# Five 64-row second parts and the skip term on the full height of the array, in a fused ConvNeXt and selective-scan kernel

## The reference, cut to what matters

```
xz = ln(silu(norm(x))) @ in_proj_w;  xc, z = split(xz)      # 192 channels each (DN)
xc = silu(conv3x3(xc) + conv_b)
xs = four orders of xc's 64 pixels (K = 4)
x_dbl = einsum('bkdl,kcd->bkcl', xs, x_proj_w)              # sum over the 192 channels
delta = softplus(dts @ dt_w + dt_b);  A = -exp(A_logs)
h = h * exp(delta * A) + (delta * u) * B;  y = sum_n h * C  # 16 states per channel
y = y + D * xs;  y = y0 + y1 + y2 + y3                      # D * xs is the skip term
y = ln(y) * silu(z);  out = y @ out_proj_w                  # mean, variance and product over 192 channels
```

## Time and profile before

| | |
|---|---|
| time, median of 3 runs | 31036.96 us (31032.65 to 31046.93) |
| span of the profiled execution | 31035.4 us |
| what lies around the span, by the median | 1.6 us |
| TensorE matmuls busy | 28615.5 us, 92% |
| VectorE busy | 27602.9 us, 89% |
| ScalarE busy | 24152.4 us, 78% |
| GpSimd busy | 25853.7 us, 83% |
| mean granted TensorE clock | 0.991 |

### The profile page before, as it was taken

One profiled execution on the slowest core, in us unless ns is written; L12 is line 12 of the kernel. 1 busy time (PEld: TensorE's weight loads), 2 busy tenths in 40 slices (PEclk: granted clock), 3 DMA queues, 4 the chain that ended last, 5 costly groups with the idle time before them and its releaser, 6 DMA issues.

```text
span 31035.4 us, 986155 instructions
## 1 busy us (share of the span) xinstructions
PE 28615.5 (92%) x399070; PEld 10807.2 (35%) x399070; DVE 27602.9 (89%) x18447; ACT 24152.4 (78%) x37826; POOL 25853.7 (83%) x13288
## 2 busy tenths in 40 slices
PE   8999799999999999999999999999999999999998
PEld 2333233333333333333333333333333333333333
DVE  7888799999999999999999999999999999999998
ACT  4555688888888888888888888888888888888887
POOL 0000599999999999999999999999999999999999
PEclk9999999999999999999999999999999999999999
DMA  3333344444444444444444444444444444444444
GB/s 82 88 84 82 79 103 99 102 98 102 99 101 100 100 100 100 101 100 102 99 102 100 101 99 101 99 103 98 103 98 102 100 102 99 102 98 102 98 102 90
DMA packets 3821867, 3043.32 MB, mean 98 GB/s; under 512 B 2184848, under 2 KB 2987792, under 8 KB 3796944
## 3 DMA queue, kind: packets, MB, share of 16 engines
q1 hardware_dynamic: 3809888, 2910.77, 44.4%
q0 software_dynamic: 8560, 77.41, 0.7%
HBM read 2325.71 MB, written 449.58 MB: 89 GB/s over the span
## 4 chain that ended last, share of the span: by engine, by line
PE 28%; POOL 20%; issue 18%; ACT 13%; DVE 8%; DMA 1%; POOLq 0%; SPq 0%; ACTq 0%; DVEq 0%
POOL state L942 17%; PE dbu L1032 9%; PE pp L1126 7%; DVE state L1477 5%; ACT state L1256 5%; PE yb L1051 4%; DVE dg L1467 2%; PE pp L1100 2%; POOL dd L949 2%; PE pp L1089 1%; PE pp L1120 1%; ACT sp_w L1333 1%; POOL dd L962 1%; ACT sp_v L1334 1%; PE b_t L1068 1%
## 5 line engine op out<-in xcount | busy, mean ns | idle before, releaser
L942 POOL TENSOR_TENSOR state<-state,cc 128x1024 f32<-128x1024 f32 x9408 | 22044.2, 2375 | 1411.5 <-DVE state L1477 1381.9
L1477 DVE TENSOR_TENSOR_SCAN state<-state,dbu 128x1024 f32<-128x1024 f32 x9408 | 21000.9, 2269 | 2295.8 <-PE dbu L1032 2292.6
L1256 ACT ACTIVATE state<-dl,a_neg 128x512 f32<-128x512 f32 x18816 | 12250.6, 711 | 21.2 <-DMA dl<-dlx 1.4
L1032 PE MATMUL dbu<-dg,du_t 64*32 64x256 f32 x301056 | 10198.2, 383 | 968.5 <-DVE state L1477 895.6
L1032 PEld LDWEIGHTS dbu<-dg,du_t 64*32 64x32 f32 x301056 | 5100.0, 106 | 7276.9 <-issue 6198.1
L1051 PE MATMUL yb<-state,mask 128*32 128x512 f32 x37632 | 5078.5, 612 | 2.2 <-POOL state L942 2.2
L1467 DVE TENSOR_TENSOR dg<-b_t,mask_q 128x1024 f32<-128x1024 f32 x3136 | 3757.7, 1198 | 41.4 <-PE b_t L1068 41.4
L229 POOL DMA_DIRECT2D act_d<-acted x32 | 16.3, 509 | 3218.2 <-DVE mixed L489 2909.2
L1126 PE MATMUL pp<-sp_a,minus 128*128 128x512 f32 x2352 | 1321.4, 644 | 587.4 <-ACT ye L1284 252.1
L1339 ACT ACTIVATE sp_y<-pp 128x512 f32<-128x512 f32 x1176 | 704.2, 599 | 1440.4 <-PE pp L1126 1417.1
L437 DVE SCALAR_TENSOR_TENSOR acc<-image,cw_v,acc 96x432 f32<-96x432 f32 (+2 forms) x2912 | 1687.6, 647 | 0.0
(11 more groups left out here) (174 smaller groups left out, 26584.2 us busy)
## 6 DMA issues: line engine op xcount, KB each, us to landing
dl<-dlx SPq DMA_DIRECT2D x4704, 256.0 KB, 4.7
cc<-cd SPq DMA_DIRECT2D x3136, 256.0 KB, 6.2
dlx<-dd SPq DMA_DIRECT2D x1176, 256.0 KB, 2.0
shifted<-in_x SPq DMA_DIRECT2D x384, 392.0 KB, 12.5
xs<-ye SPq DMA_DIRECT2D x1176, 112.0 KB, 2.8
xs<-ye SPq DMA_DIRECT2D x588, 128.0 KB, 2.6
image<-in_x SPq DMA_DIRECT2D x32, 1176.0 KB, 24.5
act_d<-acted POOLq DMA_DIRECT2D x32, 1176.0 KB, 9.1
```

The source lines that it names most:

```text
L942: nc.gpsimd.tensor_tensor(its, its, cc[:, h, s, :], ALU.mult).then_inc(hc_done, 1)
L1032: last = nc.tensor.matmul(dst[:, :, TQ * e:TQ * e + TQ], du_t[its, j, col:col + JC], dg[its, h, 2 * k + s, MG * TQ * g:MG * TQ * g + MG * ...
L1256: nc.scalar.activation(state[:, slot, :, m * WPX:m * WPX + WPX].rearrange("p (q k) t -> p q k t", k=2), by_place(dl[:, J // 2, 2 * h + J % ...
L1477: nc.vector.tensor_tensor_scan(its, its, dbu[p % 2][:], 0.0, ALU.mult, ALU.add).then_inc(scan_done, 1)
```

## The change

The weights of the second parts are stored on 128 rows, with zeros in rows 64 to 127, and the second matmuls run over all 128 rows. The other operand (`u`, `yf`, `ye1`) has 128 rows in memory already; what stands in rows 64 to 127 is multiplied by zero. The number of matmuls and their columns stay. In the setup, two buffers are cleared in addition (`out_l`, `skip_l`), half of the new second plane of `mean_y` is cleared after one more wait, and the weight loads wait for three cleared buffers, not two.

```diff
-N_CONSTS = 34 + 128 // TQ
+N_CONSTS = 37 + 128 // TQ
-        mean_y = sb("mean_y", [128, 128])
+        mean_y = sb("mean_y", [128, 2, 128])
-        skip_l = sb("skip_l", [JB, NJ, JB])
+        skip_l = sb("skip_l", [128, NJ, JB])
-                sp.wait_ge(consts, 2)
+                sp.wait_ge(consts, 3)
-                for buf, v in ((dt_l, 0.0), (xp_l, 0.0), (center, -1.0 / C), (mean, 1.0 / C), (mean_y, 1.0 / DN),
+                for buf, v in ((dt_l, 0.0), (xp_l, 0.0), (out_l, 0.0), (center, -1.0 / C), (mean, 1.0 / C),
...
-                               (zi, 0.0)):
+                               (zi, 0.0), (mean_y, 1.0 / DN), (skip_l, 0.0)):
                     nc.gpsimd.memset(buf[:], v).then_inc(consts, 1)
                     n += 1
+                pool.wait_ge(consts, n)
+                nc.gpsimd.memset(mean_y[JB:128, 1, :], 0.0).then_inc(consts, 1)
+                n += 1
...
                             last = nc.tensor.matmul(bank[JC * m:JC * m + JC, its],
                                                     skip_l[:, J // 2, JC * (J % 2):JC * (J % 2) + JC],
-                                                    u[0:JB, J // 2, its], start=False, stop=False)
+                                                    u[:, J // 2, its], start=False, stop=False)
...
-                    last = nc.tensor.matmul(pp[:], xp_l[0:JB, f, 1, :], u[0:JB, 2, :], start=False, stop=True)
+                    last = nc.tensor.matmul(pp[:], xp_l[:, f, 1, :], u[:, 2, :], start=False, stop=True)
...
-                    for part, (rows, _) in enumerate(PARTS):
-                        last = nc.tensor.matmul(pp[:], mean_y[0:rows, :], yf[0:rows, part, :], start=part == 0, stop=part == 1)
+                    for part in range(2):
+                        last = nc.tensor.matmul(pp[:], mean_y[:, part, :], yf[:, part, :], start=part == 0, stop=part == 1)
...
-                        last = nc.tensor.matmul(pp[:], mean_y[0:rows, :], ye1[0:rows, 2 + part, :], start=part == 0,
+                        last = nc.tensor.matmul(pp[:], mean_y[:, part, :], ye1[:, 2 + part, :], start=part == 0,
...
-                        last = nc.tensor.matmul(pp[0:C, :], out_l[0:rows, part, :], yf[0:rows, part, :], start=part == 0,
+                        last = nc.tensor.matmul(pp[0:C, :], out_l[:, part, :], yf[:, part, :], start=part == 0,
...
-                nc.vector.tensor_tensor(skip_l[:], ident[0:JB, 0:JB].unsqueeze(1).broadcast_to([JB, NJ, JB]),
+                nc.vector.tensor_tensor(skip_l[0:JB, :, :], ident[0:JB, 0:JB].unsqueeze(1).broadcast_to([JB, NJ, JB]),
```

## The result

The changed kernel took 30988.53 us, median of 20 runs (30974.52 to 30995.62), the kernel before in the same comparison 31042.06 us. The ratio is 0.9983, 95% interval [0.9977, 0.9989]: 0.17% faster, about 53 us. Forecast were 30937 us and 100 us. The sign was right. The time lies in the wide range of 30890 to 31045 us, but outside the 30915 to 30959 us which the forecast named for itself: the wide range held it because it also covers the cases without gain. About half of the gain is missing, so the size needs an explanation.

A forecast was written before the change was run, and what follows sets the result against it. It took a ring of waits through TensorE, VectorE, GpSimd and ScalarE as the bound, no single engine. 0.40 us (`x_dbl`) + 0.11 us (skip) = 0.51 us a tile x 196 = 100 us, giving 30937 us; range 30890 to 31045.

The forecast's parts named there:

- wide range: Whole kernel: 30890 to 31045 us, from one more hidden piece counting up to the cases without gain.
- The price of a second part: TensorE's `x_dbl` pairs: both halves at 128 rows take 1.91 us instead of 2.11, saving 0.20 us each.
- its rival: TensorE's pairs: weight loads not hidden, nothing of the 0.20 us comes; 31037 or 31015 us; chance 14 in 100.
- The skip term: Six times a tile on TensorE: entry 0.11 us shorter; only step 16's on the path, 0.11 us a tile.
- The three y pieces: `y_mean` (step 25), `y_var` (30), `y_out` (38): each saves TensorE 0.20 us, none on the path, counted 0.
- `x_dbl` at step 44: TensorE, step 44: 0.20 us saved, on the path, because ScalarE waits for the end of the second half.
- `x_dbl` at step 32: TensorE, step 32: 0.20 us saved, on the path to scan 38, which waited 2.05 us for TensorE.
- "The tile" as one tile: The sum: one walked tile's saving of 0.51 us taken 196 times, giving 100 us.
- one of the two `x_dbl` is off the path: Steps 32 and 44: one saving doesn't count, leaving the forecast within 62 us of no change; 2 of its 70.
- The clock rival: TensorE: longer gaps let its clock fall; 31211 us with a fall in every second tile; chance 3 in 100.
- GpSimd as the bound: From step 33 on GpSimd bounds, so only the skip's 0.11 us counts: 22 us, 31015 us; chance 8 in 100.

The follow-up runs named there:

- y_only: Changed kernel with `x_dbl` and the skip term back at 64 rows, so only `y_mean`, `y_var`, `y_out` on 128: 31039.26 us, ratio 1.0001 against the kernel before.
- x1_only: Kernel before with only the `x_dbl` of step 44 on 128 rows: 30994.43 us, ratio 0.9987 against the kernel before.
- the two pairs without late ones: Kernel before and changed kernel, both with the `cc` transfer made small (31010.05, 30940.62 us) or split and issued early (31005.63, 30938.34 us).
- before_small: Kernel before, moving only one window of eight of C's transfer needed at step 4 (layer not computed): 31010.05 us, ratio 0.9989.
- after_small: Changed kernel with the same small transfer of C (layer not computed): 30940.62 us, ratio 0.9967 against the kernel before.
- the early pair: Kernel before and changed kernel, both with C's transfer split by step, first part issued ahead of SyncE's wait for `dlx`: 31005.63 and 30938.34 us.
- after_early: Changed kernel with C's transfer split by step, first part issued ahead of SyncE's wait for `dlx`: 30938.34 us, ratio 0.9967 against the kernel before.

## Why the prediction was half right, by its steps

- **The price of a second part, 0.20 us: right.** 2.11 became 1.92 us. The weight load is hidden at 128 rows as the earlier trace rows said: the second half starts 0.97 us behind the first and lasts 0.95, with weights of its own. The Trainium skill's rule in "TensorE: Matmul & The Clock Gate", section "Part 3: Packing small matmuls — row/col tiling", that it overlaps only for other row groups, does not fit these rows. The same section also says that a load into the background weight buffer is pulled ahead, and the rows agree with that sentence; the prediction drew its rival from the first one alone.
- **The skip term, 0.11 us at step 16, nothing elsewhere: right.** 0.13 us measured, since the way from the skip to `x_in` is 0.02 us shorter too, and no price for the lost overlap.
- **The three y pieces at nothing: right** (y_only).
- **`x_dbl` at step 44, 0.20 us: right** (x1_only, 0.20 us).
- **`x_dbl` at step 32, 0.20 us: the step that failed first.** The forecast said that VectorE takes the earlier inputs at once, because scan 38 waits 2.05 us. That wait bounds what can be gained at its own place, not what reaches it. Between the two lie five steps in which VectorE has no gap and TensorE may be only two ahead. At step 37 TensorE had 0.08 us left to that limit, and 0.08 us is what `x_dbl` paid: 0.12 x 196 = 24 us less. With the 0.02 us more of the skip, 0.41 us add up; the medians of the tile give 0.42 us, x 196 = 82 us.
- **"The tile" as one tile: the second failure.** The sum took one clean tile 196 times. About one tile in ten of the kernel before was late at step 4 already, and the room for `cc` was 0.6 us in the median tile. The two traces have 29 late tiles for 17 and lose 28 us by them; the two pairs without late ones put the change at 67 and 69 us for 53, so by the medians some 15 us went there. What the late tiles cost scatters from trace to trace (26 tiles and 23 us in y_only, whose tile did not change), so one trace proves little about the size. The pairs carry this, and by their medians: the intervals of the single ratios, 0.0006 to 0.0012 to either side, are wider than those 15 us.
- **What stays open.** Between the 82 us of the undisturbed tiles and the 67 to 69 us of the pairs lie about 15 us. Transfers late at step 24 have about 8 us of it in both pairs (15.0 for 7.2 us, 9.2 for 0.8). The tiles of the traces don't show a loss of that size: the 185 tiles of before_small and after_small differ by 81 us, those of the early pair by 72, where 0.42 x 185 is 78. The rest is of the size of the scatter. Why the wait for `dlx` takes 4 to 5 us in some tiles isn't settled, but much of it goes with the turn of TensorE's loop: 17 of the 29 late tiles of the changed kernel come right behind a tile in which it turned. The tiles at that place are 1.1 us longer than the undisturbed one, 0.27 before and 0.00 in after_early.
- **The wide range was luck in part.** The forecast gave 2 of its 70 in 100 to the case that one of the two `x_dbl` is off the path, and something near this case came; the late tiles stand nowhere in its sum.
- **The clock rival fell** (0.991 in both), and GpSimd as the bound fell too: the 0.2 us of x1_only would not have come.

## What to carry to other kernels

If a short matmul of 64 rows stands beside full ones, zero rows in its weights are free. Each change of size that they took away here saved 0.1 us where 32 columns of the array were used and 0.2 us where it was 128. They save nothing where the change only moves to the other side, because the neighbour there has the same 64 rows and the same columns (the skip term at steps 6 and 14). Before a saving is multiplied, follow it to the wait that it should shorten, past every place where the engine may not run further ahead, and look at how many tiles aren't like the one you walked. A transfer that is "hidden" has a margin in microseconds; write it down, with all that stands ahead of it in its queue. Here it was 0.6 us, and a wait ahead of it in the queue that was 1.4 us longer in some tiles was enough.

## What the runs showed beyond that

Each eighth tile of the kernel before was 3.7 us longer, 24 times in a run, 89 us in all; with a loop body of 16 tiles on TensorE 44 us went (30938.34 to 30893.97).

TensorE's timeline of the kernel before shows the turn in one of these tiles:

```profile
9214.22 1.10 PE L1032 MATMUL dbu<-dg,du_t 64*32 64x256 f32 x32 [2.99 <-DVE dg L1467]
```

It is the first work of TensorE behind the turn, the inputs of step 1. The median wait there is 3.0 us in the tiles with a turn, 3.7 us with the loop body of 16 tiles, and nothing in the others. The view names VectorE's `dg`, but in a tile without a turn (scan 0 at 9494.31) the same inputs start 1.5 us before that `dg` begins, so they don't need it: the wait is that of the turn. What it is made of, no run here shows. The turn of a long unrolled loop on the busiest engine cost more than the whole change brought here. And rows 96 and 128 count as one size, while 64 rows next to 128 rows are another.
